# Second attention of a two-layer network: q and k in two float32r parts, two heads' scores in the two halves of TensorE's rows, maxima per quarter of the queries

## The reference, cut to what matters

```python
q = (x @ wq.T + bq)   # k, v alike; 16 heads of 16; rotary on q and k
att = jnp.einsum('bhtd,bhsd->bhts', q, k) / np.sqrt(hd)
att = jnp.where(causal, att, -jnp.inf)
att = jax.nn.softmax(att, axis=-1)
y = jnp.einsum('bhts,bhsd->bhtd', att, v)
```

## Time and profile before

| | us |
|---|---|
| median of 3 runs | 4158.48 |
| runs | 4147.53 to 4164.63 |
| span of the profiled execution, first to last instruction | 4106.3 |
| layers phase, up to its last work | 1115 |
| second attention, waiting for its first load | 46 |
| row scores of group 0 | 104 |
| groups 0 to 14 | 1745 |
| group 15 | 87 |
| experts and combine | 1009 |

### The profile page before, as it was taken

One profiled execution on the slowest core, in us unless ns is written; L12 is line 12 of the kernel. 1 busy time (PEld: TensorE's weight loads), 2 busy tenths in 40 slices (PEclk: granted clock), 3 DMA queues, 4 the chain that ended last, 5 costly groups with the idle time before them and its releaser, 6 DMA issues. The chain is left out here.

```text
span 4106.3 us, 65569 instructions
## 1 busy us (share of the span) xinstructions
PE 3499.3 (85%) x20499; PEld 1877.5 (46%) x20500; DVE 2863.1 (70%) x5100; ACT 1766.9 (43%) x2274; POOL 745.4 (18%) x968
## 2 busy tenths in 40 slices
PE   5777777777359999999999999999997999999954
PEld 2333333343113333333333333333335888888943
DVE  5777776776468777788778778787724665566556
ACT  2333333333103665666566566566673332233211
POOL 0333323233112222100000000000002121111066
PEclk9899888888658999999999999999998999999977
DMA  2121221212232221123333212223002121121077
GB/s 70 45 79 57 67 83 41 82 51 68 78 75 45 48 47 35 25 41 47 48 46 48 48 26 41 39 41 48 7 7 90 58 71 61 66 67 62 32 204 215
DMA packets 261897, 247.41 MB, mean 60 GB/s; under 512 B 92530, under 2 KB 233970, under 8 KB 261306
## 3 DMA queue, kind: packets, MB, share of 16 engines
q1 hardware_dynamic: 245178, 209.58, 21.8%
q0 software_dynamic: 16384, 33.64, 2.8%
HBM read 149.70 MB, written 92.67 MB: 59 GB/s over the span
## 5 line engine op out<-in xcount | busy, mean ns | idle before, releaser
L1313 DVE TENSOR_REDUCE at_part<-at_p 128x1 f32<-128x512 f32 (+3 forms) x2560 | 1402.1, 605 | 310.4 <-PE at_p L1197 192.2
L1294 ACT ACTIVATE at_ex<-at_st 128x1024 f32<-128x1024 f32 (+1 forms) x1280 | 1109.3, 895 | 830.8 <-PE at_st L1220 472.5
L1197 PE MATMUL at_p<-at_ks,at_qs 96*128 96x512 bf16 (+3 forms) x2560 | 838.3, 366 | 89.6 <-DVE at_part L1313 32.8
L1217 PE MATMUL at_st<-at_qs,at_ks 99*128 99x512 bf16 (+3 forms) x2560 | 713.3, 350 | 6.5 <-ACT at_ex L1294 4.9
L1234 PE MATMUL at_ob<-at_ex,at_vs 128*32 128x512 f32 (+3 forms) x5120 | 588.3, 541 | 3.6 <-ACT at_ex L1294 3.5
L1197 PEld LDWEIGHTS at_p<-at_ks,at_qs 96*128 96x128 bf16 x2560 | 248.1, 98 | 688.5 <-DVE at_part L1313 490.4
L1475 POOL DMA_INDIRECT e_xg<-s_xn,e_table x128 | 146.9, 1148 | 1978.2 <-DMA e_table<-s_table 1405.2
L1565 ACT ACTIVATE e_hh<-e_hb,e_b1now 128x512 fp32r<-128x512 f32 x256 | 176.3, 689 | 527.5 <-PE e_hb L1500 498.9
L1217 PEld LDWEIGHTS at_st<-at_qs,at_ks 99*128 99x128 bf16 x2560 | 242.0, 99 | 252.2 <-ACT at_ex L1294 97.8
L1530 PE MATMUL e_ob<-e_w2h,e_hh 128*128 128x256 f32 x1024 | 295.1, 288 | 15.5 <-DVE e_og L1623 15.5
L1532 PE MATMUL e_ob<-e_w2h,e_hl 128*128 128x256 f32 x1024 | 291.7, 285 | 0.0
(11 more groups left out here) (180 smaller groups left out, 4706.9 us busy)
## 6 DMA issues: line engine op xcount, KB each, us to landing
s_qk<-a_piece SPq DMA_DIRECT2D x192, 128.0 KB
at_qs<-s_qk SPq DMA_DIRECT2D x192, 128.0 KB
at_ks<-s_qk SPq DMA_DIRECT2D x192, 128.0 KB
s_v<-a_v SPq DMA_DIRECT2D x64, 256.0 KB, 5.5
at_vs<-s_v SPq DMA_DIRECT2D x32, 512.0 KB
e_w<-w SPq DMA_DIRECT2D x16, 1024.0 KB, 7.5
s_eo<-e_og SPq DMA_DIRECT2D x32, 512.0 KB, 2.6
a_x<-x SPq DMA_DIRECT2D x16, 512.0 KB, 5.2
```

Source lines behind the costliest of these rows:

```text
L1197: last = pe.matmul(out, qs[0:STACK, r, h, qt * P:(qt + 1) * P], ks[0:STACK, r, h, ch * SEG:ch * SEG + w], start=True, stop=not diag)
L1217: last = pe.matmul(out, ks[:, r, h, kt * P:(kt + 1) * P], qs[:, r, h, q0:q0 + w], start=True, stop=not diag)
L1294: ev.done(act.activation(ex[:, u % NE, 0:width], st[:, u % 2, 0:width], ACT.Exp, scale=SCALE), "ex")
L1313: ev.done(dve.tensor_reduce(part[:, at, ch:ch + 1], p1[:, n % NP1, 0:w], AX, ALU.max), "mx")
```

## The change

In `layers_phase`, `rot` is cut into two parts: ACT copies it to the float32r tile `part[0]`, DVE writes the difference as float32r to `part[1]`. `part1` on ACT and `last_part` on POOL are gone. SP stores two parts in eight DMAs of 256 KB, in a scratch tensor ordered by head.

In `attend_phase`:

- `qs` and `ks` are float32r, 128 partitions. Rows 0 to 49 are one head (three combinations of 16 rows and two rows for the maxima), rows 64 to 113 another. Two pairs of heads make a group. A product over 48 or 50 rows gives one head's scores; the two of a pair follow each other into two banks.
- Row scores: 80 pairs instead of 160 chunks, both into `p1`, which still has three banks, so pair k takes banks 2k and 2k+1 modulo 3. The order is by quarter of the queries. Each mask is two products of 64 columns per head.
- The maxima of a quarter are closed (DVE, 16 columns), turned, split in two and written by eight small DMAs when the quarter is done: items "t" in the stream, two pairs behind the quarter's end.
- The stream is no longer one group ahead but three quarters: while group g runs, quarter 3 of g and quarters 0 to 2 of g+1 are made. Ahead of the loop only three quarters of group 0; group 15 makes its own quarter 3.
- Key scores: a step is one key tile (in three places of a quarter a piece of one or two), a unit is a step of a pair, 72 in a group; the exponential reads two banks of `so` and is 1024 wide as before. `ex` holds four steps. Values follow in one block per step.
- On SP: the small DMAs of quarter 2, the load of g+2 (12 DMAs of 256 KB for q and k, 16 partitions each, and two for v), then the store of the last quarter of g-1, two stores of g, and so on. The last values, copy, turn and division of a group stand in the first two steps of the next one.
- Group 0 is written out, the loop holds three groups and runs four times, groups 13 to 15 are written out.

The core of the diff:

```diff
-Q_PIECES = (0, 0, 1, 0, 1, 2)
-K_PIECES = (0, 1, 0, 2, 1, 0)
+Q_PARTS = (0, 0, 1)
+K_PARTS = (0, 1, 0)
...
-                    st.mark(dve.tensor_tensor(qk[:], rot[:], piece[0][:], ALU.subtract), "rest", n)
+                    st.mark(dve.tensor_tensor(part[1][:], rot[:], part[0][:].bitcast(F32), ALU.subtract), "p2", n)
...
-                    st.mark(pool.tensor_tensor(piece[2][:], qk[:], piece[1][:], ALU.subtract), "p3", n)
...
-        qs = sb("qs", [ROWS, NBUF, G, M], BF16)
+        qs = sb("qs", [P, NBUF, PAIRS, M], F32R)
...
+        lead = stream([(0, 0), (0, 1), (0, 2)], [None, (0, 0), (0, 1)])
+        run = stream([(0, 3), (1, 0), (1, 1), (1, 2)], [(0, 2), (0, 3), (1, 0), (1, 1)])
+        tail = stream([(0, 3)], [(0, 2)]) + [("t", 0, 3)]
...
+                def row_scores(r, item, banks):
+
+                    _, _, qc, p, qt, ch = item
+                    w = wide(item)
+                    diag = ch == qc
+                    for a in range(2):
+                        rows = slice(a * HALF, a * HALF + STACK)
+                        last = pe.matmul(p1[:, banks[a], 0:w], qs[rows, r, p, qt * P:(qt + 1) * P],
+                                         ks[rows, r, p, ch * SEG:ch * SEG + w], start=True, stop=not diag)
+                        if not diag:
+                            ev.done(last, "s1")
...
+                def stream_item(g, r, use, it, n, items, k):
+
+                    item = items[k]
+                    at = 2 * (n + k)
+                    if at + 2 > NP1:
+                        ev.wait(pe, "mx", it, at + 2 - NP1)
...
-                    ev.wait(pe, "ex", g, max(u - 1, 0))
+                            if i == 0 and a == 0 and (not first or v >= PAIRS):
+                                ev.wait(pe, "ex", g, v - PAIRS + 1)
+                            rows = slice(a * HALF, a * HALF + ROWS)
+                            last = pe.matmul(so[:, b + a, at:at + w], ks[rows, r, p, kt * P:(kt + 1) * P],
+                                             qs[rows, r, p, q0:q0 + w], start=True, stop=not diag)
...
+                        ev.wait(dve, "s1", it, at + 2)
+                        ev.wait(dve, "m_in", g + ahead, G * PART * qc)
+                        ev.done(dve.tensor_copy(mT[:, 0], src), "mstep")
+                        ev.wait(dve, "mstep", g + ahead, qc + 1)
+                        dve.tensor_tensor(mT[:, 1], src, mT[:, 0].bitcast(F32), ALU.subtract).then_inc(ev.sem["mx"], 2)
```

462 lines of the change are left out of this document (239 added, 223 removed).

## The result

The changed kernel takes 4566.1 us (median of 4 runs, 4545.9 to 4591.0) beside 4161.6 for the kernel before: 1.098 times as long, interval 1.092 to 1.103. The forecast was 3959 with a range to 4130, so both the sign and the range were wrong. The profiled execution spans 4544.2 us, and its run took 4546.1. So less than 2 us lie outside a span.

The account below looks back on a forecast made before the run. PE was taken to bound the kernel before, the chain of maxima the changed one. 4106.3 - 51 (layers) - 15 (load) - 17 (group 0) - 113 (groups) - 3 (last group) = 3907, with 52 outside 3959 us; range 3850 to 4130.

Parts of the forecast that it names:

- The layers: Layers stage: without POOL's last subtraction, DVE's addition beside it and the chain behind get faster; -51 us, bounds -20 and -62.
- Group 0's row scores: Ahead of the loop: 96 maxima instead of 160, 48 pairs at half the clock; -17 us, bounds -45 and 0.
- rival (1): Row and key scores: the two halves don't run together, PE needs 31 us more a group; 4322 us, chance 0.12.
- 85% of 108.8: Fifteen groups: DVE busy near 85% of a group, as a sign in the new trace; a group about 108.8 us.
- Rival (2): SP queue: the output store waits behind the load and DVE stands 14 us a group; 4040 to 4172 us, chance 0.17.
- The load: First load of q and k, ahead of the first row score: 16 partitions instead of 8 make it quicker; -15 us.
- the prediction's 17 us: First load: by the largest-divisor rule q and k come up to twice as fast, about -17 us.
- The trips: Row scores in the groups: PE to DVE and back takes 1.26 us a pair for full tiles, a chain of 105 us.
- 39 us of values in 36 blocks: PE's need in a group: value products, with 0.1 us ahead of each block, take 39 us.
- Rival (3): Groups: PE, less busy, drops to the lower clock; 4500 us, chance 0.02.
- the groups: Fifteen groups of the attention: each takes about 108.8 us instead of 116.3, saving 113 us in all.
- the last group: Last group: 32 pairs of row scores, then ACT's pace; 84 us instead of 87, -3 us.

Follow-up runs that it names:

- e1: Changed kernel with every row-score maximum reading only the first 128 columns of its bank instead of up to 512; one run, 4239 us (4172 for the kernel before).
- e5: Changed kernel with the row scores ahead of the key scores in the first half of each step; 4411 us, 1.057 times the kernel before.
- e3: Changed kernel with each value block cut into halves of 256 query columns, the second behind the next step's first row scores; 4613 us, 1.107 times the kernel before.
- e7: Changed kernel with four more products of 512 columns ahead of each turn of the maxima, their result unused; 4666 us, 1.133 times the kernel before.
- e14: Changed kernel with single-bank waits for row scores, these first in half-steps, narrow ones spread, second key pair of one-tile steps issued twice; 1.022 times the kernel before.
- e17: Changed kernel with single-bank waits for row scores, these first in a step's first half, second key pair of one-tile steps issued twice; 1.025 times the kernel before.

## Why the prediction was wrong

**What held.** The layers: -50.8 for -51, and the addition at 1.22 us as in the one free turn of the earlier trace rows. The closeness is partly luck: the start of the last stores moved by 40.8 us where 45 were forecast, and what follows them shrank by 10 where 6 were. Group 0's row scores: -20.7 for -17. The halves run together, so rival (1) is out: pairs start within 0.02 us and the next product 0.24 later. VectorE was busy 95 us a group (1425.94 / 15), near the forecast's 85% of 108.8. Rival (2) did not bite at 146 us a group (2.4 us in all), but it is real at 127, as e1 shows (96 us in 13 waits).

**The load.** 3.3 us instead of 15. From the first load of q to the first row score it is 35.6 us (1071.5 to 1107.1) where it was 44.6, so 9 us were won, and 5.7 of them lost again, since more now stands ahead of the loads on SP: the masks in four pieces, and the six writes of ones, which took 0.95 and 0.92 us before.

```profile
1065.71 5.75 SPq L1132 DMA_DIRECT2D at_ks<-at_ex  x6
1071.51 4.37 SPq L1141 DMA_DIRECT2D at_qs<-s_qk  x6
```

That is SP's timeline in the changed kernel; its first load of q is issued 12.3 us behind the first routing load, and before it was 6.6 (1109.99 to 1116.60). And 9 is not 15:

```profile
1116.60:1161.20 44.60, 1.48 (x3) 0.43 (x4) 11.35 (x20) 0.63 (x1) 0.00 (x0) 0.50 0.58 109
```

```profile
1071.50:1107.10 35.60, 1.87 (x4) 0.44 (x4) 8.32 (x15) 0.00 (x0) 0.00 (x0) 0.50 1.00 136
```

Before, then after: the DMA engines are busy 100% of the time instead of 58%, and move 136 GB/s instead of 109, so 1.7 times the busy share made 1.25 times the speed. The Trainium skill's rule of the largest divisor (DMA: Bandwidth & Descriptors, Why a DMA increments its semaphore by 16 and not by 1) is about how many engines take part. The busy shares agree with it; the prediction's 17 us took the speed to follow, and it did not.

**The trips: the step that failed first.** The prediction put 1.26 us for each trip since "between two pairs it has 0.9 us for a key pair (0.23) and a value block (0.65), which fits for full tiles". But a full value block is 1.00 us, as its own say, a key pair behind it takes 0.34, and both stand ahead of the row scores in one of two gaps. The 0.65 is in no row; the prediction's own 39 us of values in 36 blocks are 1.08 a block. The trip is 1.28 in one gap and 1.67 in the other: 11 us a group, 160 in all. e5 shows it by moving two blocks, which takes 5 of the 11 away; even then PE needs 1.42 us for a row pair and a value block, more than the trip of 1.26.

**The clock: the step that failed most.** Rival (3) was named, with 4500 us, close to the 4566 measured, and a chance of 0.02. The price stands there without a working, so its closeness is luck. Two sentences carried the chance. "In the layers it holds 0.88 at 71% busy" compares one busy share with another, though the layers' work is another: runs of products with a long wait between (4.94 us in the earlier trace rows), not pairs that each end in a trip. "At half pace PE would be busy throughout and rise again" is refuted: 91% busy for 44 us at 0.50 in the changed kernel, 98% for 30 us in e3. The row that spoke for the rival was on the page: group 0's row scores, 100 us at 0.50 with PE 78% busy, a stream of the same products and trips that the change now sets through all groups. It was cited and then argued away, though the same prediction put group 0's new row scores at the lower clock. Measured, the clock was 0.77 in the groups, and that is 26 us a group, 390 in all.

**The sum.** 3959, plus 15 x 36.9 = 554 for the groups, plus 27 for the last group, plus 12 for the load, less 4 for group 0 and 3 for the combine stage is 4545; the profiled execution took 4546. The groups' 554 are some 165 by the trips and 390 by the clock.

**What stays open.** Why the clock stays down while the profile shows TensorE busy, and why products ahead of the turns made it worse (e7). The split into 11 and 26 us rests on the straight line, since no run holds the clock at the full level with the same work. No version was ahead of the kernel before: the nearest, e14 and e17, are 2.2 and 2.5% behind it.

## What to carry to other kernels

A change that halves TensorE's work in a stage where it is the bound can cost more than it saves. Here one engine at the full clock became two that wait for each other, at a clock that fell to 1.2 GHz for nearly half of the time. Look in the trace for a stretch where the new pattern already runs, and take its clock as the forecast unless something in the change removes it. With three buffers for units of two, let each unit wait for its own buffer, and put what feeds the other engine right behind the long block (together 7 points of the 10 lost here). Between two waits on an in-order queue, count each block that stands there at its full length.

## What the runs showed of the hardware

- Two products on rows 0 to 63 and 64 to 127 start within 0.02 us of each other (1280 pairs of row scores) and cost one: 512 columns in float32r every 0.24 us for the pair.
- TensorE's clock stayed at 1.2 GHz for 44 us with PE 91% busy, and for 30 us with 98%. Repeating 14 us of products a group raised the mean clock from 0.77 to 0.90 and made the kernel 156 us faster (ratio 1.098 to 1.056).
- The same work with value blocks of two steps together lowered the clock from 0.77 to 0.72, and brought the falls from 65 to 176 in groups 1 to 14.
- 12 loads of 16 partitions instead of 24 of 8 kept the DMA engines busy 100% instead of 58%, and moved 136 GB/s instead of 109.
- VectorE's addition of 128x1024 float32 took 4.69 us beside a subtraction on GpSimd and 1.22 without it.
- The combine stage, untouched, took 196 us in one execution and 245 in another, at 215 and 173 GB/s.
